# Two graph layers, software-pipelined by hand: another statement order on four engines and another table of PSUM places

## The chip, the cores and the metric

One NeuronCore of a Trainium2 chip runs the kernel; the other cores are idle. The metric is the device time of one launch in microseconds (us). TensorE is called PE below, VectorE DVE, ScalarE ACT, GpSimd POOL and SyncE SP, as in the profile.

## What is computed

Input: 128 graphs of 128 tokens with 384 features each (`x`), and for each graph a 128 x 128 adjacency matrix of zeros and ones (`adj`). A graph layer L0 (two rounds, l = 0 and 1), a residual with a layer norm, an attention layer L1 with 12 heads of 32, and again a residual with a layer norm:

```python
for l in range(2):                                   # L0
    m_left, m_right = h @ W_left[l].T, h @ W_right[l].T
    u_left, u_right = h @ m_left.T / temper, h @ m_right.T / temper
    u = u_left * adj_tri + u_left * diag_mask + u_right * adj_tri.T
    a = exp(u) * adj
    ctx = (a / (sum(a) + 1e-10)) @ (h @ W_lin[l].T + b_lin[l])
    h = relu(layer_norm(ctx, ln_a[l], ln_b[l]))
x = layernorm(x + h)
q, k, v = x @ Wq.T, x @ Wk.T, x @ Wv.T + bv          # L1
p = softmax(q @ k.T * scale + 2 * adj)
x = layernorm(x + (p @ v) @ Wo.T + bo)
```

All products are wanted nearly as exact as float32. The kernel makes each from three f16 matmuls (high by high, high by low, low by high parts), so every operand of a matmul is first split: ACT rounds it (`_hi`), DVE or POOL takes the rest (`_lo`).

## The kernel before

**Tiles and passes.** Four graphs make a group, so there are 32 groups. One pass of the program (`body(p)`, written out once for each engine) does L0 of group p and L1 of group p-1, so that one layer's products fill the time in which the other layer waits for its elementwise work. There are 34 passes: pass 0 has no L1, pass 32 no L0, pass 33 only the end of the last group's L1. Passes 3 to 30 run in a hardware loop with four passes in its body, so each engine jumps back at the end of passes 6, 10, 14, 18, 22 and 26.

**Steps.** On PE a pass consists of `nl` (h by W_left and W_right, transposed, 6 products of nine 512-column matmuls for each l), `hl` (h by W_lin, 4 products of nine 384-column matmuls), `u` (2), `ctx` (4 of three matmuls with float32 operands), `th` (3 groups of four float32 transposes of the normalized `z`), `x1t` (the same of `x1`), `qk` (6 of nine 512-column matmuls), `v` (4), `scores(b, c)` (for graph b and three head columns c, 12 small matmuls each that use 32 rows of the array each, four at a time), `pt` (four transposes of the weights `w` of the softmax, three groups for each graph), `pv` (36 matmuls of 33 columns), `to` (three transposes of `o`) and `po` (the output product). In full each pass has 774 matmuls.

**What sets the order.** Nothing but the text: on each engine the statements of `body` run in the order written, and semaphores make an engine wait for what another has to give. An engine that waits holds up everything that is written behind the wait. For a PE product the wait is for its operands' `_lo` parts and for its PSUM bank: `BANK_USES` lists for each of the eight banks which products use it in a pass and in what order, and `await_bank` waits until the use before has been read.

**The chains that the prediction speaks of.**

- `th(0)` on PE transposes `z`, which DVE's `norm_z` (L1017) has scaled in place. Before it come, on DVE, `bn` (L970), `z_variance` (L985, L987), then POOL's power `z_power` (L431), then DVE's `inv_std` (L1004 to L1009). Ahead of those stands `ctx(0, 3)` on PE, whose bank ACT scales into `z`.
- `to(1)` on PE transposes `o`, which DVE makes from `pv(1)`: `rs_of` (a reciprocal L874 and a product with `live`, L877), then `pv` (L889).
- `nl(1, 0)` on PE needs `hT_lo` (DVE's `th`, L1038), one third before each three of its matmuls.
- `ctx(1, 0)` on PE needs `e_lo`: `u` (PE), `u_add` (DVE), `exp_u` (ACT), `weigh` (POOL), `round_e` (ACT), `e_rest` (POOL, L427).
- `scores(b, j)` on DVE (L847) reads the scores with the adjacency added, and writes the maxima `nmax`; POOL's `folds` (L464, L472) sums the scores, and DVE's `live_of` (L865) uses both.

Line L1251 is the one matmul statement of all nl, hl, qk, v, ctx and po products, L1261 that of all transposes, L1379 that of the scores, L1312 that of u and L1405 that of pv. L537 is ACT's copy for all `_hi` parts, L812 and L814 are DVE's subtraction for the `_lo` parts.

Of the kernel before, what the change touches and what calls it, by code (L numbers as in the profile page):

```python
# [1548 lines left out]
```

How the kernel before makes its waits and increments, by code:

```python
            def await_apart(self, eng, sig, n):  # L219
                value = sig.upto(self.group(sig), n)
                if not isinstance(value, int):
                    value = eng.snap(eng.to_reg(value), min_val=1)
                eng.wait_ge(sig.sem, 1)
                eng.wait_ge(sig.sem, value)
# [1 line left out]
            def await_bank(self, eng, stage, *parts):  # L228
                last = {}
                for i in parts:
                    _, order, n = place(stage, i)
                    candidates = [(self, m) for m in range(n - 1, -1, -1)]
                    if self.before:
                        candidates += [(self.before, m) for m in range(len(order) - 1, -1, -1)]
                    for run, m in candidates:
                        if run.has(order[m]):
                            name, j = order[m]
                            group = run.group(READ[name]) - (1 if (name, j) in TAIL else 0)
                            if j >= last.get(name, (0, -1))[1]:
                                last[name] = group, j
                            break
                for name, (group, j) in last.items():
                    eng.wait_ge(READ[name].sem, READ[name].upto(group, j + 1))
# [27 lines left out]
        @block.sync  # L272
# [3 lines left out]
            for m in range(10):  # L276
                if m >= 3:
                    sp.wait_ge(w_lo_ok, m - 2)
                sp.dma_start(stage_w[m % 3], weights[m]).then_inc(w_in[m % 3], 16)
# [1232 lines left out]
            def head():  # L1512
                pe.wait_ge(const_ok, 3)
                pe.wait_ge(ones_ok, 7)
```

## Time and profile before

| | |
|---|---|
| median of 3 runs | 2906.12 us (2905.11 to 2912.86) |
| the profiled execution's own time | 2910.63 us |
| span of that execution's instructions | 2908.9 us |
| PE busy | 2811.0 us (97%) |
| DVE busy | 2433.9 us (84%) |
| ACT busy | 1773.5 us (61%) |
| POOL busy | 1662.0 us (57%) |

How to read it: the span runs from the first to the last instruction that was profiled, and everything below is told against it. A matmul's recorded duration covers its way through the array, while the next one starts as soon as its columns are in. So of PE the starts count: the distance from one start to the next is what a matmul costs, and a distance above the usual one is lost time, of which the "idle before" of a row shows only a part. Times in the rows are from the start of the span.

### The profile page before, as it was taken

The numbers are of one execution on the slowest core, as the hardware profiler recorded it, in microseconds if no ns is written. First come the engines' busy times: TensorE is split into PE (matmuls) and PEld (weight loads), VectorE is DVE, ScalarE is ACT, GpSimd is POOL, SyncE is SP. The second block draws the span as 40 slices with busy tenths as digits, with TensorE's granted clock in tenths as the row PEclk, the third lists the DMA queues.
The fourth block names the chain that finished last, engine by engine and source line by source line (L and its number), as shares of the span: only waits on it lengthen the run. The fifth ranks groups of instructions, "written<-read, shape, count | busy, mean of one in ns | idle before, by whom it ended". The sixth has DMA issues, their size and how long they took to land.

```text
span 2908.9 us, 74992 instructions
## 1 busy us (share of the span) xinstructions
PE 2811.0 (97%) x24768; PEld 1794.6 (62%) x24768; DVE 2433.9 (84%) x8042; ACT 1773.5 (61%) x4107; POOL 1662.0 (57%) x2097
## 2 busy tenths in 40 slices
PE   7999999999999999999999999999999999999996
PEld 4566666666666566665666656666566656666654
DVE  4888988888888789887888878897888888888886
ACT  4565666556676556665566655566565666655664
POOL 2555566556565556664565645656555655556564
PEclk9999999999999999999999999999999999999997
DMA  4001011101011010111110110101101011101000
GB/s 149 30 31 45 21 45 42 42 32 45 21 42 42 32 45 21 45 42 38 36 42 24 43 43 31 45 21 46 39 34 43 31 35 42 42 31 45 21 27 21
DMA packets 56061, 113.03 MB, mean 39 GB/s; under 512 B 4944, under 2 KB 37712, under 8 KB 55632
## 3 DMA queue, kind: packets, MB, share of 16 engines
q1 hardware_dynamic: 55632, 107.76, 11.0%
q8 instruction: 214, 3.51, 0.5%
q14 instruction: 215, 1.76, 0.2%
HBM read 82.58 MB, written 25.17 MB: 37 GB/s over the span
## 4 chain that ended last, share of the span: by engine, by line
PE 80%; DVE 10%; issue 6%; ACT 3%; DVEq 0%; POOL 0%; DMA 0%; SPq 0%; POOLq 0%; ACTq 0%
PE psum L1251 58%; PE psum L1261 9%; PE psum L1312 9%; PE psum L1405 3%; DVE z L1017 2%; PE psum L1379 1%; ACT w L597 1%; DVE nT_lo L814 1%; DVE rs L877 1%; DVE pT_lo L812 1%; DVE hT_lo L1038 1%; DVE o L889 1%; ACT qk_hi L537 1%; ACT pT_hi L537 1%; DVE st L916 1%
## 5 line engine op out<-in xcount | busy, mean ns | idle before, releaser
L597 ACT ACTIVATE w<-s,nmax 128x128 f32<-128x128 f32 x1536 | 479.4, 401 | 1.9 <-DVE nmax L847 1.9
L1251 PE MATMUL psum<-hT_hi,w_hi 128*128 128x512 f16 x1152 | 442.8, 384 | 35.4 <-issue 19.7
L1251 PE MATMUL psum<-hT_hi,w_lo 128*128 128x512 f16 x1152 | 442.3, 384 | 0.0
L1251 PE MATMUL psum<-hT_lo,w_hi 128*128 128x512 f16 x1152 | 442.2, 384 | 0.0
L537 ACT ACTIVATE nT_hi<-psum 128x512 f16<-128x512 f32 x384 | 230.1, 599 | 306.1 <-PE psum L1251 306.1
L847 DVE CUSTOM_DVE_ANT_0 s<-psum,adj 128x128 f32<-128x128 f32 x1536 | 350.6, 285 | 33.3 <-PE psum L1379 30.6
L464 POOL TENSOR_TENSOR fold<-fold 128x384 f32<-128x384 f32 (+4 forms) x640 | 344.0, 538 | 50.2
L464 POOL TENSOR_TENSOR fold<-s 128x768 f32<-128x768 f32 x128 | 244.2, 1908 | 194.7 <-DVE nmax L847 194.7
L388 POOL TENSOR_TENSOR hl_lo<-hl_raw,hl_hi 128x384 fp32r<-128x384 f32 x256 | 246.6, 968 | 144.9 <-ACT hl_hi L537 140.7
L812 DVE TENSOR_TENSOR pT_lo<-psum,pT_hi 128x512 f16<-128x512 f32 x384 | 251.5, 683 | 35.1 <-ACT pT_hi L537 34.7
L537 ACT ACTIVATE pT_hi<-psum 128x512 f16<-128x512 f32 x384 | 221.7, 596 | 84.3 <-PE psum L1261 84.3
L814 DVE SCALAR_TENSOR_TENSOR nT_lo<-psum,nT_hi 128x512 f16<-128x512 f32 x384 | 256.3, 681 | 12.4 <-ACT nT_hi L537 12.3
L431 POOL TENSOR_TENSOR yrstd<-yvar,pw 128x4 f32<-128x4 f32 x32 | 32.4, 1013 | 397.8 <-DVE yvar L997 397.8
L537 ACT ACTIVATE z<-psum,rden 128x384 f32<-128x384 f32 x256 | 138.3, 579 | 197.4 <-DVE rden L963 197.4
L1251 PE MATMUL psum<-w_hi,hT_lo 128*128 128x384 f16 x768 | 250.3, 326 | 0.0
L1251 PE MATMUL psum<-w_lo,hT_hi 128*128 128x384 f16 x768 | 250.3, 326 | 0.0
L1251 PE MATMUL psum<-w_hi,hT_hi 128*128 128x384 f16 x768 | 250.3, 326 | 0.0
L1251 PE MATMUL psum<-xT_hi,w_hi 128*128 128x512 f16 x576 | 219.8, 382 | 0.0
L1251 PE MATMUL psum<-xT_lo,w_hi 128*128 128x512 f16 x576 | 219.1, 380 | 0.0
L1251 PE MATMUL psum<-xT_hi,w_lo 128*128 128x512 f16 x576 | 218.8, 380 | 0.0
L1251 PEld LDWEIGHTS psum<-hT_hi,w_hi 128*128 128x128 f16 x1152 | 113.2, 98 | 165.1 <-issue 43.0
L1261 PE MATMUL psum<-ident,w 128*128 128x128 f32 x1536 | 208.7, 276 | 2.6 <-DVE nmax L847 2.0
(133 smaller groups left out, 8066.6 us busy)
## 6 DMA issues: line engine op xcount, KB each, us to landing
xTin<-xT SPq DMA_DIRECT2D x32, 768.0 KB, 4.5
xres<-x SPq DMA_DIRECT2D x32, 768.0 KB, 4.6
out<-y SPq DMA_DIRECT2D x128, 192.0 KB, 1.9
adjn<-adj SPq DMA_DIRECT2D x32, 256.0 KB, 4.8
...
```

What stands on the lines that cost most here:

```text
L388: nc.gpsimd.tensor_tensor(hl_lo[:, b, 0:FEAT], hl_raw[:, b], hl_hi[:, b, 0:FEAT].bitcast(f32), ALU.subtract).then_inc(hlr_lo[l].sem, 1)
L464: nc.gpsimd.tensor_tensor(fold[:, :, 0:n], src[:, :, 0:n], src[:, :, n:2 * n], ALU.add)\
L537: return nc.scalar.activation(dst, src, ACT.Copy, scale=scale)
L597: last = nc.scalar.activation(w[:, m], s[b % 2][:, m], ACT.Exp, bias=nmax[b % 2][:, m:m + 1], scale=-1.0)
L812: nc.vector.tensor_tensor(dst, src, rounded, ALU.subtract).then_inc(done.sem, 1)
L814: nc.vector.scalar_tensor_tensor(dst, src, scale, rounded, ALU.mult, ALU.subtract)\
L847: last = nc.vector.tensor_tensor_reduce(out=s[b % 2][:, m], in0=psum[:, SC[j], c * TOK:(c + 1) * TOK], in1=adj2[:, b], scale=-1.0 / TEMPER ...
L1017: nc.vector.tensor_scalar(z[:, b], z[:, b], rstd[0][:, b:b + 1], nmr[:, b:b + 1], ALU.mult, ALU.add)\
L1251: last = mm(dst, a, b, start=(i == 0), stop=(i == total - 1))
L1261: last = transpose(dst[:, n * 128:(n + 1) * 128], src, ident[:])
L1312: last = mm(dst, a, m, start=(i == 0), stop=(i == len(terms) - 1))
L1405: last = mm(dst[:, n * VCOL:(n + 1) * VCOL], a, m, start=(i == 0), stop=(i == 2))
```

## The change

It changes the order of the statements in the `body` of PE, ACT, DVE and POOL, and the table `BANK_USES`. Every statement that was there is there once; the operations, their sizes and the order on SP stay. In two places code is added: DVE's `scores(b, 0)` also waits for `live_ok` of the graph two before (its own `live_of`), `await_bank` takes `also`, and with it PE's `scores(0, 0)` waits for `qkr_lo` in the same wait as for its banks.

```diff
         BANK_USES = (
-            uses(("nl0", 1), ("hl0", 2), ("v", 0), ("pt", 1), ("pv", 0), ("nl1", 4), ("to", 1), ("pv", 2), ("c1", 0)),
...
+            uses(("pv", 3), ("nl0", 3), ("u0", 0), ("hl0", 2), ("qk", 0), ("v", 0, 2), ("pt", 0, 3, 4), ("nl1", 5),
                  ("pt", 9)),
...
+            uses(("nl0", 2, 4), ("hl0", 3), ("s", 1, 5), ("nl1", 2), ("s", 9, 13), ("pt", 8), ("pv", 2),
+                 ("c1", 0, 2)),
+            uses(("po", 3), ("qk", 1), ("s", 2, 6, 10, 14), ("hl1", 1), ("pt", 10), ("c1", 1, 3)),
...
-            def await_bank(self, eng, stage, *parts):
-
-                last = {}
+            def await_bank(self, eng, stage, *parts, also=()):
+
+                last = {name: (self.group(READ[name]), i) for name, i in also}
...
                 if b >= 2:
                     if j == 0:
                         p.await_apart(dve, fold1, b - 1)
+                        p.await_apart(dve, live_ok, b - 1)
...
                 if c == 0:
-                    p.await_bank(pe, "s", *range(TILES * b, TILES * (b + 1)))
-                if b == 0:
+                    p.await_bank(pe, "s", *range(TILES * b, TILES * (b + 1)), also=(("qk", 1),) if b == 0 else ())
+                elif b == 0:
```

The body of PE from `qk(0)` on, before and after, several statements to a line (the engines' other bodies are reordered in the same way):

```
before: qk0 qk1 | ctx(0,0) ctx(0,1) | qk2 | ctx(0,2) ctx(0,3) | qk3 qk4 qk5 | v0 | th0 | scores(0, all) | th1 | v1 v2 v3 |
        th2 | scores(1, all) | pt(0,0) pt(0,1) | nl(1,0) nl(1,1) | pt(0,2) pt(1,0) | nl(1,2) | pv0 | nl(1,3) |
        scores(2, all) | to0 | nl(1,4) | pt(1,1) pt(1,2) | po0 | nl(1,5) | pv1 | hl(1,0) | scores(3, all) | to1 |
        hl(1,1) | pt(2, all) | u(1,0) | po1 | pv2 | u(1,1) | pt(3,0) | to2 | hl(1,2) | pt(3,1) | hl(1,3) | pt(3,2) |
        po2 | ctx(1,0) ctx(1,1) ctx(1,2) ctx(1,3)
after:  qk0 | ctx(0,0) ctx(0,1) | qk1 | ctx(0,2) ctx(0,3) | qk2 qk3 qk4 qk5 | th0 | v0 | scores(0,0) scores(0,1) | th1 |
        scores(0,2) | v1 v2 v3 | scores(1,0) scores(1,1) | th2 | scores(1,2) | pt(0, all) | nl(1,0) nl(1,1) | pt(1,0) |
        nl(1,2) | pv0 | nl(1,3) | scores(2, all) | to0 | pt(1,1) pt(1,2) | nl(1,4) | po0 | pv1 | scores(3, all) |
        nl(1,5) | pt(2,0) | hl(1,0) | pt(2,1) | hl(1,1) | pt(2,2) | u(1,0) u(1,1) | pt(3,0) | to1 | pv2 | pt(3,1) |
        hl(1,2) | po1 | to2 | hl(1,3) | pt(3,2) | ctx(1,0) ctx(1,1) | po2 | ctx(1,2) ctx(1,3)
```

Ahead of that PE's `hl(0, 1)` moves behind `u(0, 0)` and `u(0, 1)`, `hl(0, 2)` ahead of `x1t`, and `po(3)` behind `nl(0, 5)`.

The first place is DVE ahead of `th(0)`, in a pass of the loop. Before, from the row behind the variance L987 on (L814 with `qk_lo` is `qk`, L931 `fin(3)`, L1004 to L1009 `inv_std(0)`, L1017 `norm_z`):

```order
L804 REGISTER_ALU
L814 SCALAR_TENSOR_TENSOR qk_lo<-psum,qk_hi 128x512
L804 REGISTER_ALU
L814 SCALAR_TENSOR_TENSOR qk_lo<-psum,qk_hi 128x512
L804 REGISTER_ALU
L814 SCALAR_TENSOR_TENSOR qk_lo<-psum,qk_hi 128x512
L931 SCALAR_TENSOR_TENSOR nmr2<-mv2,rstd2 128x1
L1003 REGISTER_ALU
L1004 TENSOR_SCALAR sd_eps0<-sd0 128x4
L1006 RECIPROCAL rstd0<-sd_eps0 128x4
L1009 SCALAR_TENSOR_TENSOR nmr<-mv0,rstd0 128x4
L1017 TENSOR_SCALAR z<-z,rstd0,nmr 128x384 x4
```

The same place on DVE after the change (its lines are three further down; L934 is `fin(2)`):

```order
L990 TENSOR_SCALAR var0<-mv0 128x4
L934 SCALAR_TENSOR_TENSOR nmr2<-mv2,rstd2 128x1
L805 REGISTER_ALU
L815 SCALAR_TENSOR_TENSOR qk_lo<-psum,qk_hi 128x512
L1006 REGISTER_ALU
L1007 TENSOR_SCALAR sd_eps0<-sd0 128x4
L1009 RECIPROCAL rstd0<-sd_eps0 128x4
L1012 SCALAR_TENSOR_TENSOR nmr<-mv0,rstd0 128x4
L1020 TENSOR_SCALAR z<-z,rstd0,nmr 128x384 x4
L805 REGISTER_ALU
L815 SCALAR_TENSOR_TENSOR qk_lo<-psum,qk_hi 128x512
```

Between the variance and `norm_z` one `qk_lo` stands instead of three; the other two come behind `norm_z`.

The second place is PE behind `scores(3, 2)`, before:

```order
L1379 MATMUL psum<-qk_hi,qk_lo 128x128 x4
L1261 MATMUL psum<-ident,o1 128x128 x3
L1251 MATMUL psum<-w_hi,hT1_hi 128x384
L1251 MATMUL psum<-w_lo,hT1_hi 128x384
L1251 MATMUL psum<-w_hi,hT1_lo 128x384
```

and the place in which the same transposes `to(1)` of `o1` stand after the change:

```order
L1315 MATMUL psum<-nT_hi,hT1_lo 128x256
L1264 MATMUL psum<-ident,w 128x128 x4
L245 REGISTER_ALU
L1264 MATMUL psum<-ident,o1 128x128 x3
L245 REGISTER_ALU
L1408 MATMUL psum<-v_hi,pT0_hi 128x33
```

`to(1)` stood directly behind the scores and now stands behind `u(1, 1)` and `pt(3, 0)`, with nine other products in between.

The third place is PE at the end of a pass, before:

```order
L1251 MATMUL psum<-w_hi,oT0_hi 128x384
L1251 MATMUL psum<-w_lo,oT0_hi 128x384
L1251 MATMUL psum<-w_hi,oT0_lo 128x384
L1251 MATMUL psum<-hl_hi,e_hi 128x386
L1251 MATMUL psum<-hl_lo,e_hi 128x386
L1251 MATMUL psum<-hl_hi,e_lo 128x386
```

and after:

```order
L1264 MATMUL psum<-ident,w 128x128 x4
L1254 MATMUL psum<-hl_hi,e_hi 128x386
L1254 MATMUL psum<-hl_lo,e_hi 128x386
L1254 MATMUL psum<-hl_hi,e_lo 128x386
L245 REGISTER_ALU
L1254 MATMUL psum<-hl_hi,e_hi 128x386
L1254 MATMUL psum<-hl_lo,e_hi 128x386
L1254 MATMUL psum<-hl_hi,e_lo 128x386
L1254 MATMUL psum<-w_hi,oT0_hi 128x384
L1254 MATMUL psum<-w_lo,oT0_hi 128x384
L1254 MATMUL psum<-w_hi,oT0_lo 128x384
```

`ctx(1, 0)` and `ctx(1, 1)` now come ahead of `po(2)`; `ctx(1, 2)` and `ctx(1, 3)` stay behind it and, by the new table, use the banks of the first two again.

## Rows read from the trace of the kernel before

**Rows 1.** Page, part 4: chain that ended last, share of the span by engine

```profile
PE 80%; DVE 10%; issue 6%; ACT 3%; DVEq 0%; POOL 0%; DMA 0%; SPq 0%; POOLq 0%; ACTq 0%
```

**Rows 2.** Waits of PE: line, waited for: us in total, times, longest

```profile
PE psum L1261 <- DVE o L889: 25.4, 36, 4.1
PE psum L1251 <- issue: 20.0, 7, 4.4
PE psum L1261 <- DVE z L1017: 14.2, 32, 6.0
```

**Rows 3.** Stretches (passes 0, 13, 32): us, busy PE PEld DVE ACT POOL, clock, DMA

```profile
11.77:77.25 65.48, 56.36 (x289) 32.08 (x289) 34.73 (x61) 31.34 (x51) 21.60 (x24) 0.90 0.32 106
1136.91:1224.62 87.71, 86.85 (x776) 55.78 (x775) 75.74 (x252) 54.86 (x128) 51.89 (x66) 1.00 0.11 37
2827.72:2896.43 68.71, 49.62 (x488) 30.52 (x488) 50.35 (x196) 34.78 (x87) 30.53 (x43) 0.80 0.05 17
```

**Rows 4.** Timeline, pass 13, PE and DVE at th(0): start us, us, what

```profile
1175.06 0.69 DVE L814 SCALAR_TENSOR_TENSOR qk_lo<-psum,qk_hi 128x512 f16<-128x512 f32 x1 [0.66 <-ACT qk_hi L537]
1176.34 1.65 DVE L1017 TENSOR_SCALAR z<-z,rstd,nmr 128x384 f32<-128x384 f32 x4
...
1177.31 0.33 PE L1251 MATMUL psum<-w_lo,xT_hi 128*128 128x384 f16 x1
1177.47 0.33 PE L1251 MATMUL psum<-w_hi,xT_lo 128*128 128x384 f16 x1
...
1178.05 0.66 PE L1261 MATMUL psum<-ident,z 128*128 128x128 f32 x4 [0.25 <-DVE z L1017]
```

**Rows 5.** The same timeline a little later: the last scores and the next transposes

```profile
1179.09 0.22 PE L1379 MATMUL psum<-qk_hi,qk_lo 32*128 32x128 f16 x4
...
1179.24 0.66 PE L1261 MATMUL psum<-ident,z 128*128 128x128 f32 x4
```

**Rows 6.** Timeline, pass 13, around scores(3) and to(1)

```profile
1205.10 1.16 POOL L380 TENSOR_TENSOR hT_lo<-xTin,hT_hi 128x512 f16<-128x512 f32 x1
...
1205.23 1.04 DVE L877 SCALAR_TENSOR_TENSOR rs<-live,rs 128x12 f32<-128x12 f32 x1
...
1205.51 0.33 PE L1251 MATMUL psum<-w_hi,hT_lo 128*128 128x384 f16 x1
1205.77 0.23 PE L1379 MATMUL psum<-qk_hi 32*128 32x128 f16 x4
...
1206.23 0.22 PE L1379 MATMUL psum<-qk_hi,qk_lo 32*128 32x128 f16 x4
...
1206.99 0.55 PE L1261 MATMUL psum<-ident,o 128*128 128x128 f32 x3 [0.55 <-DVE o L889]
```

**Rows 7.** Timeline, pass 32: the last scores and a V product behind them

```profile
2862.32 0.22 PE L1379 MATMUL psum<-qk_hi,qk_lo 32*128 32x128 f16 x4
2862.47 0.34 PE L1251 MATMUL psum<-w_hi,xT_hi 128*128 128x384 f16 x1
```

**Rows 8.** Timeline, pass 13, inside nl(1, 0)

```profile
1187.28 0.38 PE L1251 MATMUL psum<-hT_hi,w_lo 128*128 128x512 f16 x1
...
1187.72 0.39 PE L1251 MATMUL psum<-hT_hi,w_hi 128*128 128x512 f16 x1
```

**Rows 9.** Timeline of PE where the loop begins again: pass 7, pass 19

```profile
611.66 0.54 PE L1261 MATMUL psum<-ident,o 128*128 128x128 f32 x3 [1.27 <-DVE o L889]
...
1674.33 0.60 PE L1251 MATMUL psum<-hT_hi,w_hi 128*128 128x512 f16 x1 [4.39 <-issue]
```

**Rows 10.** Timeline, end of pass 13: to(2), e_rest, ctx(1, 0), ACT's first ctx copy

```profile
1216.88 0.49 PE L1261 MATMUL psum<-ident,o 128*128 128x128 f32 x3
...
1219.78 1.42 POOL L427 TENSOR_TENSOR e_lo<-e,e_hi 128x256 fp32r<-128x256 f32 x2
...
1222.34 0.47 PE L1251 MATMUL psum<-hl_hi,e_hi 128*128 128x386 f32 x1
...
1224.62 1.05 ACT L537 ACTIVATE z<-psum,rden 128x384 f32<-128x384 f32 x2 [2.40 <-DVE rden L963]
```

More of the change, by code:

```diff
@@ L690, in body @@
                 x1_norm(p, 3)
+                setup(p, 4)
+                exp_u(p, 0, 0)
                 hl(p, 0, 0)
-                hl(p, 0, 1)
-                x1t(p, 0)
-                exp_u(p, 0, 0)
-                x1t(p, 1)
-                x1t(p, 2)
-                round_e(p, 0, 0)
-                exp_u(p, 0, 1)
-                fin(p, 2)
-                hl(p, 0, 2)
+                x1t(p, 0)
+                x1t(p, 1)
+                round_e(p, 0, 0)
+                x1t(p, 2)
+                exp_u(p, 0, 1)
+                hl(p, 0, 1)
+                hl(p, 0, 2)
+                hl(p, 0, 3)
+                round_e(p, 0, 1)
+                setup(p, 5)
+                ctx(p, 0, 0)
+                ctx(p, 0, 1)
                 qk(p, 0)
-                round_e(p, 0, 1)
-                hl(p, 0, 3)
-                ctx(p, 0, 0)
                 qk(p, 1)
-                ctx(p, 0, 1)
                 ctx(p, 0, 2)
                 ctx(p, 0, 3)
+                fin(p, 2)
                 qk(p, 2)
@@ L767, in body @@
                 round_e(p, 1, 0)
-                to(p, 2)
-                exp_u(p, 1, 1)
+                round_e(p, 1, 1)
                 hl(p, 1, 2)
-                round_e(p, 1, 1)
-                pt(p, 3, 1)
+                hl(p, 1, 3)
                 pt(p, 3, 2)
-                hl(p, 1, 3)
                 ctx(p, 1, 0)
@@ L1118, in body @@
                 hl(p, 0, 0)
+                u(p, 0, 0)
                 resid_inv(p)
+                u_add(p, 0, 0)
                 resid_norm(p, 0)
+                u(p, 0, 1)
+                resid_norm(p, 1)
+                u_add(p, 0, 1)
                 hl(p, 0, 1)
-                resid_norm(p, 1)
-                u(p, 0, 0)
-                fin(p, 2)
-                u_add(p, 0, 0)
-                u(p, 0, 1)
-                u_add(p, 0, 1)
+                hl(p, 0, 2)
                 x1t(p, 0)
@@ L1151, in body @@
                 norm_z(p, 3)
+                setup(p, 5)
+                qk(p, 3)
+                fin(p, 3)
+                qk(p, 4)
                 qk(p, 5)
                 v(p, 0)
-                setup(p, 5)
+                setup(p, 6)
+                th(p, 0)
                 scores(p, 0, 0)
@@ L1217, in body @@
[L1217 to L1218 removed]
                 hl(p, 1, 2)
                 pt(p, 3, 0)
+                pt(p, 3, 1)
+                po(p, 1)
                 hl(p, 1, 3)
[L1222 removed]
+                to(p, 2)
+                po_stats(p, 1)
+                den(p, 1, 0)
                 pt(p, 3, 2)
[L1224 to L1228 removed]
                 bn(p, 1, 0)
@@ L1230, in body @@
                 bn(p, 1, 1)
+                po(p, 2)
+                den(p, 1, 1)
+                po_stats(p, 2)
+                live_of(p, 3)
+                fin(p, 1)
+                setup(p, 9)
                 bn(p, 1, 2)
-                fin(p, 1)
                 bn(p, 1, 3)
```

231 lines of the change are left out of this document (108 added, 123 removed).

## The prediction

> **What bounds the kernel now.** I read the shares of the engines first, then the chain that ended last, then the waits of PE, then one pass in order of time. PE is busy in 97% of the span and makes 80% of the chain; DVE makes 10% of it, and 6% is issue [rows 1]. So the question is where PE stands still. Its waits, summed over the launch, are 25.4 us for DVE's `o`, 20.0 us with no releaser ("issue") and 14.2 us for DVE's `z` [rows 2]. A pass of the loop takes 87.71 us, in which PE is busy for 86.85 us at the full clock, 2.4 GHz; pass 0 takes 65.48 us and pass 32, which has L1 alone, 68.71 us [rows 3]. DVE has 75.74 us of work in a pass: little room, but it isn't the bound [rows 3].
>
> In a pass I find three places where PE's starts are further apart than they should be. A matmul of 384 columns follows the one before after 0.16 us, and the first transpose of `th(0)` comes 0.58 us after the last matmul of `v(0)`, so 0.42 us are lost [rows 4]. The cause stands on DVE: `norm_z` starts at 1176.34, behind a `qk_lo` that itself waited until 1175.06 for ACT, and so for PE's `qk(4)` [rows 4]. After the scores of graph 3 the transposes of `o` come 0.76 us after the scores' last start [rows 6]; where nothing is late that step is 0.15 us [rows 5], so 0.61 us are lost. And inside `nl(1, 0)` one step is 0.44 us where 512 columns take 0.16 x 512/384 = 0.22 us: 0.22 us lost on `hT_lo` [rows 8]. Together 1.25 us of the 87.71 us. More than that another order can't win in a pass, since the work of PE stays the same.
>
> **The change, part by part.** *`th(0)`.* PE's `ctx(0, 2)` and `ctx(0, 3)` come one 512-column product of nine earlier (1.94 us), and on DVE two `qk_lo` (0.69 us each [rows 4], and above all the wait for PE between them) move from ahead of `norm_z` to behind it. The transposes themselves come ahead of `v(0)`, nine steps of 0.16 us = 1.46 us earlier. Before, `norm_z` ended 1.65 us after 1176.34 at 1177.99. By my walk it is now ready some 0.7 us ahead of its use: gain 0.42 us.
>
> *`to(1)`.* Nine products now stand between the scores and it, so even the `rs` product of 1.04 us on DVE [rows 6], which held `pv` up, is covered several times. Gain 0.61 us. What comes up to the scores instead is `nl(1, 5)`, whose operands are long there. Late next would be `hl(1, 1)`, whose bank waits for DVE's scores(3, 2): I find 0.4 us of room.
>
> *`nl(1, 0)`.* `pt(0, 2)` stands ahead of it now and `th` on DVE runs sooner after ACT: gain 0.22 us, little room.
>
> *Scores cut in two.* For graphs 0 and 1 a `th` now stands between the scores. Going into scores costs PE 0.26 - 0.16 = 0.10 us, with some 0.01 us more in their first steps [rows 6]; the scores' own step is (1206.23 - 1205.77) / 8 = 0.06 us [rows 6], and the step from the last of them to an f16 product is 0.15 us, 0.09 us more [rows 7], to a transpose the same [rows 5]. Two more entries and two more exits: 2 x 0.11 + 2 x 0.10 = 0.42 us lost.
>
> *End of a pass.* `ctx(1, 0)` comes one `po` (1.46 us) earlier in PE's order, while the `e_rest` on which it waits can't: its `round_e` stands on ACT behind the copy of `to(2)`. Before, `to(2)` started at 1216.88, the first of two `e_rest` ended half of 1.42 us after 1219.78, so 3.61 us behind it, and `ctx(1, 0)` started at 1222.34, another 1.85 us later [rows 10]. Now `ctx(1, 0)` stands only 2.2 us behind `to(2)` (three transposes, `hl(1, 3)`, four transposes). If the 3.61 us stay, it waits 1.4 us; but they held a `u_add`, an `exp_u` and a `weigh` that come earlier now, with `u(1, 1)` two products ahead of where it was, and what is left (transposes, two copies on ACT, the `e_rest`) I put at 2.0 us. So the cost is between 0 and 1.4 us, and I take 0. `ctx(1, 2)` uses the bank of `ctx(1, 0)` again, and ACT must have copied that: ACT's first copy began 2.28 us after `ctx(1, 0)` before and takes half of 1.05 us [rows 10], 2.8 us in all, where `ctx(1, 2)` stands 1.2 + 1.46 = 2.7 us behind `ctx(1, 0)` now. Between 0 and 0.5 us; I take 0.2 us.
>
> *Added waits.* `scores(b, 0)` on DVE waits for DVE's own `live_of`, one or more statements ahead. It stands directly behind it only before scores(3, 0). The wait costs DVE between nothing and the 0.66 us that it idled for another engine [rows 4]; I take nothing, since what hides it is DVE's room there, and without that it is part of rival A. The bank table and the merged wait of scores(0, 0) cost nothing either: by the table each bank that I followed is read 0.4 us or more ahead, apart from the one just named. Of the DMAs, only adjacency for L1 starts later, since `fin(2)`, whose store is ahead of it on SP, moves back by some 9 us; by my walk it lands some 3 us ahead of the scores.
>
> *The sum for a pass:* 0.42 + 0.61 + 0.22 - 0.42 - 0.2 = 0.63 us. Passes 1 to 31 have both layers: 31 x 0.63 = 19.5 us, less 1.5 us since passes 1, 2 and 31 lack one or the other wait = 18 us.
>
> *Where the loop begins again.* PE waits up to 4.39 us for nothing that the profile shows, before its first product [rows 9], 20.0 us in seven such waits [rows 2]. That doesn't hang on the order and stays. In three of the six there comes a wait for `o` before `to(3)`, 1.27 us idle in one [rows 9], since DVE comes round late as well. DVE's `pv(3)` now comes ahead of the variance and two scalings, so `to(3)` is ready; but `u(0, 0)` and `x1t(0)` come nearer, so I take half of some 3 us: 1.5 us.
>
> *First and last passes.* The longest wait for `z`, 6.0 us [rows 2], is in pass 0, where `ctx` now comes some 1.4 us sooner; pass 32, at 0.80 of the clock [rows 3], gains under 1 us since the weights of graph 3 no longer queue behind `to(1)`. I take 3 us, between 0 and 5.
>
> *Total:* 18 + 1.5 + 3 = 22.5 us off the profiled execution's 2910.63 us. That execution is 4.5 us above the median shown, so the forecast is 2906.12 - 22.5 = 2883.6 us, say **2883 us**.
>
> At one place the Trainium skill weighs against this. In rows: `rs`, a product of two SBUF operands on DVE, took 1.04 us and ended at 1206.27, just as POOL's 1.16 us operation from 1205.10 did (1206.26) [rows 6]. The page "SBUF — State Buffer", section "Who interferes with whom", says that a DVE instruction with two SBUF inputs and a GpSimd instruction that reads SBUF exclude each other for the whole instruction, whichever came first; the trace agrees. By that rule `rs` of graph 1 loses its partner here and finds another, the folds of graph 2, and the time would be that of rival A.
>
> **The rivals.** *(A) DVE falls behind between scores(2) and `hl(1, 1)`.* It has PE's tightest row of uses there, and POOL's folds run beside `live_of`, `rs_of` and `u_add`. For it: DVE is busy for 75.74 of 87.71 us [rows 3], and one such operation grew to 1.04 us [rows 6]. Two of them would take 1.7 us where I count 0.4 to 1.1 us of room. Against it: `nl(1, 5)` gives PE 1.94 us of work that needs nothing. Price: 0.3 to 0.6 us in a pass, so 10 to 19 us back: 2893 to 2902 us.
>
> *(B) Slower: `ctx(1, 0)` waits.* If all the 3.61 us from `to(2)` to the end of `e_rest` stay [rows 10], PE stands still for 1.4 us there in each pass; from 0.63 us on the gain of a pass is gone. Price: 31 x (1.4 - 0.63) = 24 us, against 4.5 us won at the ends, so 2926 us. For it: nothing else in the new order is as near, and ACT has two `exp_u`, `fin(0)`, `xt(2)` and `pt(3, 1)` to do ahead of that copy. Against it: ACT is busy for only 54.86 us of a pass [rows 3], and waits for PE there rather than the other way round.
>
> *(C) The stalls go and the splits cost nothing.* If the exits are hidden by weight loads and `ctx(1, 2)` isn't late, all 1.25 us are won: 31 x 1.25 + 8 = 47 us at most, 2859 us.
>
> *(D) The order does nothing.* Each stall comes back at the next product, as DVE's work is the same: 2906 us less the ends, 2901 to 2906 us.
>
> **How the numbers follow.** Forecast (2873 to 2893 us) 0.52, A 0.2, B 0.1, C 0.1, D 0.08. A measurement of this kernel tells 0.3%, 9 us, from no change. Faster by more are the forecast, C and over half of A: 0.75. Within are the rest of A and D: 0.16. Slower is B with little of D: 0.09. The range leaves out B, and the far end of C: 2866 to 2903 us.
>
> **What would show it.** In the new profile a pass of the loop should take 87.0 to 87.2 us; PE's waits for `z` and for `o` should fall to little more than those of passes 0, 32 and 33; the step inside `nl(1, 0)` should be 0.22 us; the scores should show six entries in a pass. B would show as waits of PE for POOL's `e_lo` or for ACT's `z`, A as waits for `nmax` before `hl(1, 1)`, and the waits by issue should be 20 us as before. A pass over 87.7 us makes the prediction wrong.

## The result, and the profile after

| | before | after |
|---|---|---|
| median of 5 runs each | 2908.26 us (2905.11 to 2912.86) | 2921.55 us (2917.44 to 2922.63) |
| ratio, 95% interval | | 1.0043 [1.0029, 1.0058] |
| span of the profiled execution | 2908.9 us | 2915.7 us |

Every time here is of fast executions (of run 10, a single one, that can't be told); runs 5 and 9 below had a slow one each (5245.39 us at a granted clock of 0.766, 2942.42 us at 0.942), which is left out of their medians.

The change made the kernel slower by 0.43%, 13 us, where I had forecast 2883 us and a range that ended at 2903. I read the same views in the same order. First the waits of PE after the change (line, what it waited for: us in total, times, longest):

```profile
PE psum L1254 <- issue: 20.0, 6, 4.7
PE psum L1254 <- DVE nmax L850: 14.6, 28, 0.6
...
PE psum L1264 <- DVE z L1020: 6.0, 1, 6.0
PE psum L1264 <- DVE o L892: 4.8, 2, 2.6
```

The waits for `o` (L1264 <- DVE o) and `z` (L1264 <- DVE z) fell from 25.4 and 14.2 us to 4.8 and 6.0 us [rows 2], as intended, and issue is 20.0 us as before. The second line is new: in 28 passes PE waits for `nmax`, that is for DVE's `scores`. The page's chain that ended last, shares by engine:

```profile
PE 85%; DVE 9%; issue 4%; DVEq 1%; ACT 1%; POOL 0%; DMA 0%; SPq 0%; POOLq 0%; ACTq 0%
```

PE has 5 points more than before and DVE one fewer [rows 1], which by itself looks like a better kernel. But DVEq, DVE's own instruction queue, has 1% where it had 0%. Next the stretches of passes 0, 13 and 32 (columns as in [rows 3]):

```profile
11.72:77.64 65.92, 54.97 (x289) 31.56 (x289) 35.11 (x62) 31.29 (x51) 22.94 (x25) 0.90 0.32 106
1139.66:1227.82 88.16, 87.64 (x776) 55.83 (x775) 74.30 (x252) 55.14 (x128) 51.44 (x66) 1.00 0.11 37
2833.91:2902.05 68.14, 47.37 (x487) 30.15 (x487) 49.66 (x197) 34.44 (x85) 30.54 (x43) 0.82 0.05 17
```

A pass of the loop takes 88.16 us where it took 87.71 us. The recorded busy time of PE went up with it, from 86.85 to 87.64 us, though the matmuls are the same: a matmul's record covers its way through the array, so fewer and shorter gaps between records don't mean fewer lost starts. Only the distances of starts tell. Now the places that the prediction spoke of, in pass 13. PE at `th(0)`, which stands behind `qk(5)`, and DVE's `norm_z`:

```profile
1176.69 1.65 DVE L1020 TENSOR_SCALAR z<-z,rstd,nmr 128x384 f32<-128x384 f32 x4
...
1178.72 0.38 PE L1254 MATMUL psum<-xT_hi,w_lo 128*128 128x512 f16 x1
1178.94 0.60 PE L1264 MATMUL psum<-ident,z 128*128 128x128 f32 x4
1179.38 0.33 PE L1254 MATMUL psum<-w_hi,xT_hi 128*128 128x384 f16 x1
```

`norm_z` ends at 1178.34, 0.60 us ahead of its use (0.7 predicted), and the transposes start 0.22 us after a 512-column matmul, the usual step. `to(1)` starts at 1216.98 without any wait, 0.43 us behind the four transposes of `pt(3, 0)`, and all steps in `nl(1, 0)` are 0.22 us. So the three stalls of the prediction are gone. PE before `hl(1, 1)`:

```profile
1209.42 0.33 PE L1254 MATMUL psum<-w_hi,hT_lo 128*128 128x384 f16 x1
1209.58 0.60 PE L1264 MATMUL psum<-ident,w 128*128 128x128 f32 x4
1210.70 0.34 PE L1254 MATMUL psum<-w_hi,hT_hi 128*128 128x384 f16 x1 [0.52 <-DVE nmax L850]
```

Four transposes take 0.43 us, so `hl(1, 1)` starts 1.12 - 0.43 = 0.69 us late. What DVE does ahead of it (the rows of `nmax`, 0.08 us each behind every row of L850, are left out):

```profile
1205.55 0.55 DVE L919 BATCH_NORM_STATS2 st<-y 128x6 f32<-128x384 f32 x1
1206.20 0.18 DVE L921 BATCH_NORM_AGGREGATE mv<-st 128x2 f32<-128x6 f32 x1
1206.49 0.15 DVE L927 TENSOR_SCALAR var<-mv 128x1 f32<-128x1 f32 x1
1206.56 0.84 DVE L868 SCALAR_TENSOR_TENSOR live<-nmax,total 128x12 f32<-128x12 f32 x1
1207.91 0.29 DVE L850 CUSTOM_DVE_ANT_0 s<-psum,adj 128x128 f32<-128x128 f32 x1 [0.50 <-DVE live L868]
...
1208.81 0.17 DVE L880 SCALAR_TENSOR_TENSOR rs<-live,rs 128x12 f32<-128x12 f32 x1
1209.22 0.29 DVE L850 CUSTOM_DVE_ANT_0 s<-psum,adj 128x128 f32<-128x128 f32 x1 [0.24 <-issue]
...
1210.35 0.28 DVE L850 CUSTOM_DVE_ANT_0 s<-psum,adj 128x128 f32<-128x128 f32 x1
1210.57 0.55 DVE L892 TENSOR_TENSOR o<-psum,rs 128x384 f32<-128x384 f32 x1
```

Three losses stand here. `live` takes 0.84 us (graph 0's, alone, took 0.16 us) beside POOL's folds, which run from 1204.48:

```profile
1206.38 2.81 POOL L465 TENSOR_TENSOR fold<-fold 128x384 f32<-128x384 f32 x5
```

The first of these five takes 1.00 us, to 1207.38, and `live` ends at 1207.40. Then DVE stands idle for 0.50 us: `scores(3, 0)` waits for `live_ok`, the added wait, and for what its queue has to do behind it (runs 2 and 5 part the two). Then for 0.24 us ahead of `scores(3, 1)`, with no releaser. `scores(3, 2)` ends at 1210.63, and only then has `hl(1, 1)` its bank.

Smaller ones lie elsewhere. PE at `pt(1, 1)` and `pt(1, 2)`, and at `ctx(1, 0)` and `ctx(1, 2)`:

```profile
1199.62 1.25 PE L1264 MATMUL psum<-ident,w 128*128 128x128 f32 x8
1200.72 0.38 PE L1254 MATMUL psum<-hT_hi,w_hi 128*128 128x512 f16 x1
...
1223.91 0.41 PE L1254 MATMUL psum<-hl_hi,e_hi 128*128 128x386 f32 x1
1224.16 0.34 PE L1254 MATMUL psum<-hl_lo,e_hi 128*128 128x386 f32 x1
...
1226.36 0.33 PE L1254 MATMUL psum<-w_hi,oT_lo 128*128 128x384 f16 x1
1226.67 0.41 PE L1254 MATMUL psum<-hl_hi,e_hi 128*128 128x386 f32 x1
```

Eight transposes take 0.87 us elsewhere (four take 0.43 us) and 1.10 us here: `pt(1, 2)` loses 0.22 us on the bank that DVE's `scores(2, 0)` has just read. `ctx(1, 2)` starts 0.31 us behind the matmul ahead of it, a step that usually takes 0.16 us, and its own second step is 0.25 instead of 0.18 us.

**The account of a pass.** I laid the starts of all PE steps of passes 4 to 29 side by side, before and after, and took the mean of what each lost beyond its usual steps. Gone: 0.49 us (`th(0)`), 0.67 us (`to(1)`, net of the exit from the scores that `nl(1, 5)` now pays), 0.22 us (`nl(1, 0)`), 1.38 us in all. New: 0.70 us (`hl(1, 1)`), 0.48 us (scores cut in two), 0.22 us (`pt(1, 2)`), 0.22 us (`ctx(1, 2)`), 0.14 us (`ctx(1, 0)`), 0.03 us (`pt(3, 1)`), 1.79 us in all. That is 0.41 us more; the median of the 15 passes of the loop that touch no jump went from 87.72 to 88.16 us, 0.44 us more.

Over the launch that makes 29 x 0.44 = 12.8 us for passes 3 to 31. Where the loop begins again, the profiled execution of after lost 7.8 us less than that of before (27.1 against 34.9 us by which passes 3 to 31 exceed 29 steady ones), and passes 0, 1, 2, 32 and 33 cost 1.8 us more: 12.8 - 7.8 + 1.8 = 6.8 us, the difference of the spans. The profiled execution of after was the fastest of its runs, that of before 2.4 us above its median. So the medians, 13.3 us apart, are near what the passes alone explain, but how the loop's starts and the ends share in that is known for one execution of each kernel only.

### The profile page after: what moved, and what is told of

It is laid out like the page before. It is cut to its first block, busy times and chain, and to the rows that moved or that the text cites. A ratio compares the mean times of both kernels' runs of the same rounds, so it can differ in the third digit from the quotient of the medians.

```text
span 2915.7 us, 74982 instructions
## 1 busy us (share of the span) xinstructions
PE 2827.6 (97%) x24768; PEld 1794.7 (62%) x24768; DVE 2391.1 (82%) x8042; ACT 1780.3 (61%) x4107; POOL 1652.8 (57%) x2097
## 4 chain that ended last, share of the span: by engine, by line
PE 85%; DVE 9%; issue 4%; DVEq 1%; ACT 1%; POOL 0%; DMA 0%; SPq 0%; POOLq 0%; ACTq 0%
PE psum L1254 63%; PE psum L1315 9%; PE psum L1264 9%; DVE s L850 4%; PE psum L1408 3%; PE psum L1382 2%; DVE live L868 1%; DVE nmax L850 1%; DVE pT_lo L813 1%; DVE st L919 1%; DVE y L911 1%; DVEq L225 0%; DVEq L227 0%; DVE oT_lo L813 0%; DMA s<-weights 0%
## 5 line engine op out<-in xcount | busy, mean ns | idle before, releaser
L850 DVE CUSTOM_DVE_ANT_0 s<-psum,adj 128x128 f32<-128x128 f32 x1536 | 356.8, 286 | 90.5 <-PE psum L1382 65.1
L465 POOL TENSOR_TENSOR fold<-fold 128x384 f32<-128x384 f32 (+4 forms) x640 | 336.1, 525 | 50.2
L1264 PE MATMUL psum<-ident,w 128*128 128x128 f32 x1536 | 226.5, 277 | 6.6 <-ACT w L598 3.9
L1315 PE MATMUL psum<-nT_hi,hT_hi 128*128 128x256 f16 x768 | 209.4, 273 | 0.0
```

The costliest lines, as they stand in the source:

```text
L465: nc.gpsimd.tensor_tensor(fold[:, :, 0:n], src[:, :, 0:n], src[:, :, n:2 * n], ALU.add)\
L850: last = nc.vector.tensor_tensor_reduce(out=s[b % 2][:, m], in0=psum[:, SC[j], c * TOK:(c + 1) * TOK], in1=adj2[:, b], scale=-1.0 / TEMPER ...
L1264: last = transpose(dst[:, n * 128:(n + 1) * 128], src, ident[:])
L1315: last = mm(dst, a, m, start=(i == 0), stop=(i == len(terms) - 1))
```

## Experiments

All pass times below are medians of the same 15 passes of a kernel's profiled execution; "0.69 us a pass" and the like are means over passes 4 to 29. "Before" is the kernel before, run beside them: 2908.4 us in the first four runs, 2909.4 us in the next four, 2909.6 us and 2908.9 us in the rest.

### 1. Another bank for hl(1, 1)

```diff
-            uses(("nl0", 2, 4), ("hl0", 3), ("s", 1, 5), ("nl1", 2), ("s", 9, 13), ("pt", 8), ("pv", 2),
+            uses(("nl0", 2, 4), ("hl0", 3), ("s", 1, 5), ("nl1", 2), ("s", 9, 13), ("hl1", 1), ("pv", 2),
                  ("c1", 0, 2)),
-            uses(("po", 3), ("qk", 1), ("s", 2, 6, 10, 14), ("hl1", 1), ("pt", 10), ("c1", 1, 3)),
+            uses(("po", 3), ("qk", 1), ("s", 2, 6, 10, 14), ("pt", 8), ("pt", 10), ("c1", 1, 3)),
```

> The changed kernel with two places swapped in the table: hl(1,1) takes the bank of scores(3,1), pt(2,2) that of scores(3,2). Nothing else. Theory T (DVE is late at scores(3,2), and PE loses 0.69 us a pass before hl(1,1) by that alone): hl(1,1) then waits for scores(3,1), which DVE ends 0.7 us sooner, so the wait falls to 0 to 0.1 us, a pass from 88.15 to about 87.5 us, the time by 31 x 0.65 = 20 us to about 2901 us. Rival U (DVE as a whole is behind there, and the next product that needs it waits instead): a wait of the same size comes up at pt(2,2) or u(1,0), 2918 to 2922 us. Rival V (the wait before hl(1,1) isn't a bank's): nothing changes, 2921 us.

Measured: 2900.34 us, ratio to before 0.9967 [0.9955, 0.9979]; pass 87.46 us. PE at the same place:

```profile
1203.22 0.60 PE L1264 MATMUL psum<-ident,w 128*128 128x128 f32 x4
1203.65 0.33 PE L1254 MATMUL psum<-w_hi,hT_hi 128*128 128x384 f16 x1
```

The wait is gone, 0.43 us between the starts. DVE is exactly as late as in after (0.50 and 0.24 us idle), and nothing else waits for it. So theory T holds: in after, PE would reach `hl(1, 1)` at 1210.01, 4.4 us behind its last scores, and DVE frees that bank at 1210.63. This one place of the table cost 21 us. U and V fall.

### 2. live_of(1) early on DVE

```diff
+                live_of(p, 1)
                 scores(p, 2, 3)
                 po(p, 0)
                 nl(p, 1, 4)
                 po_stats(p, 0)
-                live_of(p, 1)
                 scores(p, 3, 0)
```

> The changed kernel with DVE's live_of(1) moved up, from directly ahead of scores(3,0) to ahead of scores(2,3), where POOL is idle. The added wait of scores(3,0) for live_ok stays, with two operations and po_stats between. Theory T (the end of live_of, waited for right behind it, and live_of's own 0.84 us beside POOL's folds make DVE late): live takes 0.16 us, the idle 0.50 us ahead of scores(3,0) goes, scores(3,2) ends about 1.2 us sooner, hl(1,1) doesn't wait, about 2900 us. Rival W (another DVE operation beside the folds grows in its place, po_stats or rs_of by 0.7 us): half of it comes back, hl(1,1) waits some 0.1 us or not at all, but the idle of 0.5 us goes: 2900 to 2905 us. Rival U (DVE as a whole is behind): 2918 us.

Measured: 2901.49 us, ratio 0.9974 [0.9964, 0.9985]; pass 87.47 us. DVE's rows:

```profile
1197.33 0.17 DVE L868 SCALAR_TENSOR_TENSOR live<-nmax,total 128x12 f32<-128x12 f32 x1
...
1200.14 0.15 DVE L927 TENSOR_SCALAR var<-mv 128x1 f32<-128x1 f32 x1
1200.88 0.29 DVE L850 CUSTOM_DVE_ANT_0 s<-psum,adj 128x128 f32<-128x128 f32 x1 [0.58 <-issue]
```

The time is as expected and the reason only half so. `live` takes 0.17 us, and that alone (0.67 us) brings `hl(1, 1)` its bank in time. But the idle ahead of `scores(3, 0)` didn't go. It is 0.58 us now, with no releaser, although `live` had ended 3.4 us ahead. So the 0.50 us were not simply the wait for DVE's own result. That led to theory Q, tried in runs 5 and 10.

### 3. The scores in one piece

On PE `th(1)` goes behind `scores(0, 2)` and `th(2)` behind `scores(1, 2)`.

> The changed kernel with the scores of graphs 0 and 1 in one piece again on PE: th(1) behind scores(0,2), th(2) behind scores(1,2). Theory S (each cut costs an entry of 0.07 us and an exit of 0.19 us): 2 x 0.26 = 0.52 us a pass, 31 x 0.52 = 16 us, so about 2905 us, with hl(1,1) still waiting 0.69 us. Rival (as I predicted, 0.21 us a cut): 13 us, 2908 us. Rival U (DVE as a whole is the bound, and time won on PE comes back as a longer wait before hl(1,1)): 2919 to 2922 us, with that wait at 1.2 us.

Measured: 2907.62 us, ratio 0.9995 [0.9986, 1.0004]; pass 87.67 us, 0.49 us less than after, 0.25 us a cut. `hl(1, 1)` waits 0.68 us as before: PE and DVE both come sooner by what the cuts cost, since DVE's late stretch begins with PE's `scores(2, 0)`. So DVE isn't the bound as a whole, it is late by a fixed amount.

### 4. Four things at once

Runs 1, 2 and 3 together, and at the end of the pass:

```diff
-            uses(("pv", 3), ("nl0", 3), ("u0", 0), ("hl0", 2), ("qk", 0), ("v", 0, 2), ("pt", 0, 3, 4), ("nl1", 5),
+            uses(("nl0", 0, 3), ("u0", 0), ("hl0", 2), ("qk", 0), ("v", 0, 2), ("pt", 0, 3, 4), ("nl1", 5),
...
-            uses(("nl0", 0, 5), ("u0", 1), ("qk", 3), ("s", 0, 4), ("nl1", 0), ("s", 8), ("pt", 5), ("s", 12),
-                 ("pt", 7)),
+            uses(("pv", 3), ("nl0", 5), ("u0", 1), ("qk", 3), ("s", 0, 4), ("nl1", 0), ("s", 8), ("pt", 5), ("s", 12),
+                 ("pt", 7), ("c1", 2)),
...
-                 ("c1", 0, 2)),
-            uses(("po", 3), ("qk", 1), ("s", 2, 6, 10, 14), ("hl1", 1), ("pt", 10), ("c1", 1, 3)),
-            uses(("nl0", 1), ("hl0", 0), ("x1t", 1), ("qk", 2), ("s", 3, 7, 11, 15), ("hl1", 2, 3)))
+                 ("c1", 3)),
+            uses(("po", 3), ("qk", 1), ("s", 2, 6, 10, 14), ("pt", 8), ("pt", 10), ("c1", 0)),
+            uses(("nl0", 1), ("hl0", 0), ("x1t", 1), ("qk", 2), ("s", 3, 7, 11, 15), ("hl1", 2, 3), ("c1", 1)))
...
+                round_e(p, 1, 0)
+                round_e(p, 1, 1)
                 to(p, 2)
-                round_e(p, 1, 0)
-                round_e(p, 1, 1)
```

> The changed kernel with four things at once: the bank of hl(1,1) and DVE's live_of(1) as in the two runs before, scores whole again as in the third, and at the end of a pass ctx(1,2), ctx(1,3) in banks of their own (nl(0,0) and pv(3) swap places for it) and ACT's two round_e ahead of its copy of to(2). If each loss is separate, a pass loses 0.69 + 0.52 + 0.22 (ctx(1,2)) + 0.14 (ctx(1,0)) = 1.57 us less: 86.6 us, and the time is 2921.5 - 31 x 1.57 = 2873 us. Rival U (DVE is behind as a whole): a new wait of PE for DVE of 0.5 us or more in each pass, 2885 us or more.

Measured: 2869.56 us, ratio 0.9857 [0.9842, 0.9872], 38.8 us under before. Pass 13 (columns as in [rows 3]):

```profile
1124.32:1210.94 86.62, 86.62 (x775) 55.90 (x775) 73.46 (x252) 55.11 (x128) 51.52 (x66) 1.00 0.11 38
```

86.62 us, as the sum of the separate losses said (88.16 - 1.57 = 86.59 us). The losses that the change brought are independent of one another, and so can be read one by one from the starts.

### 5. The added wait last

```diff
                 if b >= 2:
                     if j == 0:
                         p.await_apart(dve, fold1, b - 1)
-                        p.await_apart(dve, live_ok, b - 1)
                     p.await_apart(dve, p_ok, (b - 2) * TILES + j + 1)
...
                 p.await_apart(dve, s_full, b * TILES + j + 1)
+                if j == 0 and b >= 2:
+                    p.await_apart(dve, live_ok, b - 1)
```

(and the same in the branch for graphs 0 and 1).

> The changed kernel with the added wait for live_ok in scores(b, 0) put behind the waits for p_ok and s_full instead of ahead of them; nothing else. In the second run DVE's live_of(1) had moved far away, and the idle ahead of scores(3,0) stayed (0.58 us, with no releaser) though live_of's own 0.7 us went. Theory Q (it is the queue of DVE: each of the four waits there takes it about 0.16 us of instructions, and it can't run ahead of a wait for DVE's own result): with live_ok last, the work for p_ok and s_full is done under live_of's 0.84 us, the idle falls from 0.50 to 0.15-0.25 us, PE's wait before hl(1,1) from 0.69 to about 0.4 us, the time by 31 x 0.3 = 9 us to 2912 us. Rival P (it is the time from the end of live_of to its semaphore and to the next start, wherever the wait stands): 0.50 us as before, 2921 us.

Measured: 2916.80 us, ratio 1.003 [1.0019, 1.0041]; pass 87.95 us. DVE's rows:

```profile
1210.51 0.83 DVE L870 SCALAR_TENSOR_TENSOR live<-nmax,total 128x12 f32<-128x12 f32 x1
1211.49 0.29 DVE L852 CUSTOM_DVE_ANT_0 s<-psum,adj 128x128 f32<-128x128 f32 x1
```

From the end of `live` to the scores it is now 0.15 us, not 0.50, and `hl(1, 1)` waits 0.34 us. So theory Q holds and P falls: the way of the result is 0.15 us at most, and the other 0.36 us (0.51 from the end of `live` to the scores before) were the queue's work for two waits that stood behind the waiting one. The time gained less than the 9 us expected, since the same edit made `scores(2, 0)` start 0.06 us later behind PE, and `pt(1, 2)`, which waits for its bank, lose 0.38 instead of 0.22 us.

To take the wait away altogether wasn't tried: `scores` would then write `nmax` with nothing that orders it behind the reading `live_of`.

### 6 to 8. The old kernel, one stall at a time

Run 6, on DVE of the kernel before:

```diff
                 qk(p, 2)
-                qk(p, 3)
-                qk(p, 4)
-                fin(p, 3)
                 inv_std(p, 0)
                 norm_z(p, 0)
...
                 norm_z(p, 3)
+                qk(p, 3)
+                qk(p, 4)
+                fin(p, 3)
```

> The kernel before with one edit: DVE's inv_std(0) and norm_z ahead of qk(3), qk(4) and fin(3) instead of behind them. POOL's power ends 0.8 us after qk(2) there, so norm_z ends some 1.3 us sooner, ahead of th(0)'s turn. If the stalls are additive: the 0.43 + 0.06 us at th(0) go, 31 x 0.45 = 14 us, 2894 us. Rival D of the prediction (a stall that goes comes back at the next product that needs DVE): to(1) or nl(1,0) waits longer, 2905 us or more. Its waits for o stay at 25 us.

Measured: 2918.51 us, ratio 1.0033 [1.0022, 1.0045]; pass 88.05 us, 0.33 us more than in the kernel before. DVE and PE:

```profile
1178.45 0.96 DVE L1004 TENSOR_SCALAR sd_eps<-sd 128x4 f32<-128x4 f32 x1 [0.55 <-POOL sd L431]
...
1179.86 1.65 DVE L1017 TENSOR_SCALAR z<-z,rstd,nmr 128x384 f32<-128x384 f32 x4
1181.42 1.28 DVE L814 SCALAR_TENSOR_TENSOR qk_lo<-psum,qk_hi 128x512 f16<-128x512 f32 x2
...
1182.25 0.63 PE L1261 MATMUL psum<-ident,z 128*128 128x128 f32 x4 [0.34 <-DVE qk_lo L814]
```

`z` is ready at 1181.51, and yet `th(0)` starts at 1182.25: it uses the bank of `qk(3)`, which DVE now reads behind `norm_z`. The same stall has another holder, and further on the last third of graph 0's scores waits for the last `qk_lo` (0.33 us from start to start where 0.05 us is usual). Beside it a second thing was to be seen: `sd_eps` took 0.96 us where it took 0.16 us before. It now runs beside POOL's next operation (1178.39 to 1179.39) and ends with it, which I take for the cause; no run was made for that alone.

Run 7, on PE and DVE: `to(p, 1)` behind `hl(p, 1, 1)` instead of ahead of it.

> The kernel before with to(1) behind hl(1,1) instead of ahead of it, on PE and DVE. hl(1,1) comes up to the scores; its bank waits for DVE's pv(1), which ends about when PE gets there, so between 0 and 0.1 us are lost. If additive: 0.62 us a pass, less that, 31 x 0.55 = 17 us, 2891 us. Rival D: DVE, which then has hl(1,1) ahead of the copy for to(1), holds up po(1) or pv(2): 2900 us or more.

Measured: 2904.94 us, ratio 0.9984 [0.9975, 0.9993]; pass 87.67 us, 0.05 us less than before. DVE and PE:

```profile
1203.69 1.04 DVE L877 SCALAR_TENSOR_TENSOR rs<-live,rs 128x12 f32<-128x12 f32 x1
1204.84 0.56 DVE L889 TENSOR_TENSOR o<-psum,rs 128x384 f32<-128x384 f32 x1
...
1205.45 0.34 PE L1251 MATMUL psum<-w_hi,hT_hi 128*128 128x384 f16 x1 [0.54 <-DVE o L889]
```

`hl(1, 1)` waits for `o` in place of `to(1)`, since its bank is that of `pv(1)`, and it is the same instruction that reads that bank. I had expected that reading to end when PE gets there; it ended 0.6 us later, for the 1.04 us of `rs`.

Run 8, both edits.

> The kernel before with both edits of the two runs ahead. If the stalls are additive: 31 x (0.45 + 0.55) = 31 us less, 2877 us, without any cut of the scores and without new banks. Rival D: as much as the larger of the two alone, about 2891 us.

Measured: 2917.34 us, ratio 1.0034 [1.0021, 1.0047]; pass 88.01 us. In sum: in the old table both stalls have a second holder, a bank that the same late stretch of DVE sets free. Neither of these two orders takes its stall away with the old table. The change did take both away, with another order and another table together; the two weren't run apart, so that the new table was needed is argued from these banks and not shown. Runs 1 and 4 show what the change is worth without its own bank waits.

### 9 to 11. A further bank, and po_stats out of the way

Run 9 is run 4's kernel with `("pt", 5)` and `("nl1", 4)` exchanged in the table, DVE's `nl(p, 1, 4)` ahead of `po(p, 0)`, and `po_stats(p, 0)` behind `pv(p, 1)`:

> The kernel of the fourth run with two more changes. pt(1,2) and nl(1,4) swap banks, so that pt(1,2) no longer waits for DVE's scores(2,0) (0.22 us a pass), and DVE takes nl(1,4) ahead of po(0), because scores(3,0) on PE now waits for it. DVE's po_stats(0), which waits twice for its own results, moves from ahead of scores(3,0) to behind pv(1). Theory Q: the idle of 0.58 us ahead of scores(3,0) on DVE falls under 0.1 us. On PE 0.22 us go, of which scores(3,0) may lose up to 0.1 us again: 31 x 0.12 to 31 x 0.22 = 4 to 7 us, from 2869.6 to 2863 to 2866 us. Rival: the new bank of nl(1,4) makes PE wait 0.3 us or more before scores(3,0), 2872 us or more.

Measured: 2862.80 us, ratio 0.9841 [0.9828, 0.9854], the lowest median of all (that of run 11 is within its spread); but pass 86.72 us, 0.10 us more than in run 4. PE ahead of the scores of graph 3:

```profile
1184.64 0.18 PE L1408 MATMUL psum<-v_hi,pT_lo 128*128 128x33 f16 x1
1185.06 0.24 PE L1382 MATMUL psum<-qk_hi 32*128 32x128 f16 x4 [0.24 <-DVE nT_lo L815]
```

This step is usually 0.11 us and here 0.42 us: the rival came true, 0.31 us for 0.22 us won. In the passes the swap is a loss. The time fell all the same, where the loop begins again (below), so that it lies at the edge of the expected 2863 to 2866 us is luck.

Run 10 is run 2's kernel with DVE's `po_stats(0)` behind `pv(1)`:

> The second run's kernel (live_of(1) early) with DVE's po_stats(0) behind pv(1). Theory Q (the queue of DVE can't run ahead past po_stats, which waits for its own results, so the four waits of scores(3,0) come uncovered): the idle of 0.58 us ahead of scores(3,0) falls under 0.1 us, the scores start 1.6 us sooner (1.0 us of po_stats too); the idle of 0.24 us ahead of scores(3,1), behind rs_of's own wait, stays. Rival (scores(3,0) waits for something that another engine ends at that time): it goes on starting at 67.6 us from nl(0,0), with more idle. The time is that of the second run, about 2900 us, since PE doesn't wait there any more.

Measured: one run of 2909.7 us; pass 87.45 us. DVE's rows:

```profile
1203.15 0.68 DVE L815 SCALAR_TENSOR_TENSOR nT_lo<-psum,nT_hi 128x512 f16<-128x512 f32 x1
1204.14 0.29 DVE L850 CUSTOM_DVE_ANT_0 s<-psum,adj 128x128 f32<-128x128 f32 x1 [0.30 <-PE psum L1382]
...
1205.04 0.63 DVE L880 SCALAR_TENSOR_TENSOR rs<-live,rs 128x12 f32<-128x12 f32 x1
1205.59 0.28 DVE L850 CUSTOM_DVE_ANT_0 s<-psum,adj 128x128 f32<-128x128 f32 x1
```

The idle of the queue is gone: `scores(3, 0)` starts 66.28 us behind `nl(0, 0)` instead of 67.57, and what is left of idle is for PE's own scores. The idle ahead of `scores(3, 1)` went as well, which I had not expected; `rs` takes 0.63 us here beside the folds and covers the queue's work. The pass is as expected; the time isn't (2900 expected), and again it is the loop that differs.

Run 11 repeats that edit on run 4's kernel:

> The kernel of the fourth run (2869.6 us) with DVE's po_stats(0) behind pv(1), and without the swap of banks that cost 0.31 us a pass before scores(3,0). In the steady passes PE should be as in the fourth run, 86.62 us, with DVE's idle ahead of scores(3,0) near zero. The open question is where the loop begins again: PE stood there 28 us in sum above its passes in the fourth run and 18 us in the run with both edits. If the edit of DVE made those starts shorter: about 2859 us. If the swap of banks did, or chance: 2867 to 2870 us.

Measured: 2865.43 us, ratio 0.9848 [0.9834, 0.9861]; pass 86.63 us as in run 4, loop starts 26.3 us. So it is not the edit of DVE that makes them short. Whether run 9's swap of banks did, or chance, stays open. Chance in the one profiled execution isn't all of it: run 9's median is 2.6 us lower than run 11's, though its passes cost 29 x 0.09 = 2.6 us more.

### 12. The end of the pass alone

The table and the `round_e` of run 4, without the rest.

> The changed kernel with the end of the pass alone mended: ctx(1,0) to ctx(1,3) in four different banks (nl(0,0) and pv(3) swap places for it), and ACT's two round_e ahead of its copy of to(2). If the losses are additive: 0.22 us at ctx(1,2) and 0.14 us at ctx(1,0) go, 31 x 0.36 = 11 us, 2910 us, with the wait before hl(1,1) unchanged at 0.69 us. Rival: what is won at the end of a pass is lost at nl(0,0) or pv(3) of the next, 2918 to 2922 us.

Measured: 2902.97 us, ratio 0.9975 [0.9964, 0.9986]; pass 87.80 us, 0.36 us less than after, as expected, and `hl(1, 1)` still waits. The time is 7 us lower than expected: the passes explain 29 x 0.36 = 10.4 of the 18.6 us between the medians. Between the profiled executions of after and of this run, 13.4 us apart, they explain as much, the starts of the loop 2.1 us and the first and last passes 0.9 us; the other 5 us between the medians stay open.

### Where the loop begins again

Above their steady passes the profiled executions lost there 34.9 us (before), 27.1 us (after), 17.8 us (run 9, of which 1.5 us are pass 31's) and 39.7 us (run 10), over six starts. Two stretches of the last start, after: from the last matmul to the first, and the six matmuls behind it (columns as in [rows 3]; the clock is the third number from the end):

```profile
2387.44:2392.50 5.06, 0.33 (x2) 0.01 (x2) 2.57 (x10) 1.76 (x3) 4.14 (x5) 0.93 0.18 50
2392.50:2395.03 2.53, 2.53 (x6) 0.88 (x7) 0.00 (x0) 0.00 (x0) 0.00 (x0) 0.50 0.05 16
```

The same in run 9:

```profile
2342.79:2344.97 2.18, 0.34 (x3) 0.02 (x2) 1.94 (x10) 1.05 (x2) 0.94 (x3) 1.00 0.00 0
2344.97:2347.50 2.53, 2.53 (x32) 1.46 (x33) 0.93 (x2) 0.71 (x1) 2.53 (x3) 1.00 0.29 87
```

After, PE stood for 5.06 us and then ran at 0.50 of the clock, 1.2 GHz: six matmuls in 2.53 us. In run 9 it stood for 2.18 us and went on at 2.4 GHz. So a start costs its stand, 2 to 5 us, and up to 1.9 us more when the first nine matmuls are slow. The length of the stand alone doesn't decide whether they are: the first start of run 11 stood for 2.22 us and its matmuls then came 0.43 us apart (1.2 GHz), the second of after stood for 3.24 us and went on at 0.22 us a matmul. In run 9 five of the six stands are 2.2 to 2.5 us, in run 10 all six 4.7 to 5.1 us. What makes the stands long in one kernel and short in another I didn't find; it moves the total by 10 us or more, about as much as the effect that I had to predict.

## Why the prediction was wrong

**Right.** Where the stalls were, what held them first (runs 6 to 8 show a bank as the second holder of two of them), and that they would go: 0.49, 0.67 and 0.22 us measured, against 0.42, 0.61 and 0.22 us. The cut scores: 0.48 us against 0.42 us. `ctx(1, 2)`: 0.22 us against 0.2 us. Issue: 20.0 us. The late item next in line was named as well, `hl(1, 1)` with the bank of `scores(3, 2)`.

**Wrong, 0.70 us a pass.** "Late next would be `hl(1, 1)`, whose bank waits for DVE's scores(3, 2): I find 0.4 us of room", and, of the added wait, "I take nothing, since what hides it is DVE's room there". I added DVE's operations at the lengths they have elsewhere. Three things were not in that walk, and runs 2, 5 and 10 measured each: `live_of(1)` moved beside POOL's folds and took 0.84 instead of 0.16 us; the queue's work for the four waits of `scores(3, 0)` came uncovered, 0.50 to 0.58 us; and that for two waits ahead of `scores(3, 1)`, 0.24 us. Before, `scores(3, 0)` stood behind `pv(1)` and `hl(1, 0)`, and DVE had no idle time there:

```profile
1206.38 0.56 DVE L889 TENSOR_TENSOR o<-psum,rs 128x384 f32<-128x384 f32 x1
1206.86 0.55 DVE L827 SCALAR_TENSOR_TENSOR hl_raw<-psum,bias 128x384 f32<-128x384 f32 x1
1207.32 0.28 DVE L847 CUSTOM_DVE_ANT_0 s<-psum,adj 128x128 f32<-128x128 f32 x1
```

The three make 0.68 + 0.50 + 0.24 = 1.4 us, and from 0.4 us of room to 0.7 us of wait it is 1.1 us, so the rest of the walk had DVE some 0.3 us later than it was. The mechanism is rival A, and its sign came, waits for `nmax` before `hl(1, 1)`. Its chance of 0.2 was too small, and its price of 0.3 to 0.6 us too low: I had put two stretched operations into it and none of the queue, and there were one and the queue. In rows: it was `live` that met the folds, and it ended with the first of them. I had written that by the Trainium skill's rule (the page "SBUF — State Buffer", section "Who interferes with whom") `rs` would find another partner; `live`, with `nmax` and `total` both in SBUF, is under the same rule, and the trace agrees with it by its 0.84 us.

**Wrong, 0.22 us a pass.** "by the table each bank that I followed is read 0.4 us or more ahead". I had not followed `pt(1, 2)`, which uses the bank of `scores(2, 0)`.

**Wrong, 0.14 us a pass.** `ctx(1, 0)`: I took 0 of a range up to 1.4 us. `e_rest` ends just behind its turn; rival B was the right place with a tenth of its size.

Together: 0.63 us forecast as a gain, + 0.13 us (the stalls were larger) - 0.70 - 0.22 - 0.14 - 0.06 (cuts) - 0.02 (`ctx(1, 2)`) - 0.03 (`pt(3, 1)`) = 0.41 us lost, against 0.44 us measured.

**The ends.** I forecast 4.5 us won there. Passes 0 to 2, 32 and 33 cost 1.8 us instead, and the loop starts, 7.8 us less in the profiled execution, differ as much between the kernels of the experiments. (One slip in the chances: "slower" got 0.09 as "B with little of D", where B alone had 0.1.)

**Rival D**, that a stall which goes comes back at the next product, has its real form in runs 6 to 8: not the next product by order, but the next one that shares a bank with what is late.
